# Half of the query projection moved from the last key tile to the second of the query stages

## The chip, the cores and the metric

The kernel runs on one core of one Trainium2 chip. The metric is the device time of one execution in microseconds (us). Before the change it is 979.66 us, the median of three runs (974.97 to 980.01).

## The reference, cut to what matters

One decoder layer, batch B = 2, 1024 tokens, width 256: random-feature attention, then cross attention, then a causal attention with eight chosen experts per head. Each part reads a layer norm of x and adds its result to x. The change lies in the first part:

```python
q = split_heads(x @ Wq.T + bq)
k = split_heads(x @ Wk.T + bk)
v = split_heads(x @ Wv.T + bv)
logits = einsum('bhld,hdf->bhlf', k, W0) - 0.5 * sum(k * k)
alpha = softmax(logits over all L * NF)      # over all tokens and features
N = einsum('bhlf,bhld->bhfd', alpha, v)      # sums of the key features
D = sum(alpha, axis=2)
phi = softmax(einsum('bhld,hdf->bhlf', q, W0))
out = (phi @ N) / (phi @ D + EPS)
```

Sixteen heads of 16 columns, 64 features a head. The query projection `x @ Wq.T + bq` gives a 256 x 1024 matrix for each batch.

## The kernel before, in words

The program has a hand-written order for each engine, and semaphores between them. For each of the two batches (loop over b) the first attention runs so:

- Key projection: `projection` (L1101 to L1107) makes one piece n of four (256 columns of output in two halves, 1024 tokens in two chunks of 512). A piece is two float32 matmuls of 128x512, which the profile shows as four instructions.
- Key tiles, t = 0 to 7 (from L1147): the features of 128 keys (L1153), their values (L1161), some of the squares of the keys (L1167, one semaphore `kk_ps` at the end of tile 7), and, by the table `QUERIES_AT` (L243), pieces of the query projection (L1171 to L1175): piece 0 with tile 3, piece 1 with tile 4, pieces 2 and 3 with tile 7. All four use bank 7 of PSUM, so a piece waits until ScalarE has moved the one before out of it (`until(pe, "q_sb", b, n)`).
- VectorE takes maxima and subtracts them (L834, L842). After tile 7's maxima it makes the weights of the keys (L824, L825), GpSimd takes a maximum across the partitions (L498), VectorE subtracts it (L849), ScalarE takes exp (L616), and VectorE multiplies the values by the weights in two parts (L880; the first part covers ten heads).
- ScalarE moves the projections into `kqT` and adds the bias in `biased` (L568 to L573; the activation is L572). Inside the key loop (L610 to L620) it moves the first piece of a tile ahead of the exp L616, the second behind the exp L618 of the same tile. `kqT` lies in the tile that the profile calls region.
- Query stages, s = 0 to 25 (L1193). In stage s TensorE makes the features f of query tile s (L1207), turns the exp of the tile before (L1222), multiplies the tile two back by the sums (L1255), and so on down a chain of lags. Stages 0 and 1 also hold the sums of the key features, N and D, in two halves of 64 matmul instructions each (L1239). L1239 waits for the exp of all key tiles and for its part of the weighted values.
- In stage 2 the sums are put in place. ScalarE copies them (L649), TensorE turns them (L1214), then turns the exp of query tile 1 (L1222), VectorE copies the turned sums into windows (L889, L891, six copies, semaphore `n_blk`), TensorE multiplies them by a small block (L1228, `za_ps`), VectorE adds that (L922, `n_ready`), and TensorE may begin L1255 for query tile 0. VectorE has the subtraction L914 of query tile 2 between the last copy and L922.
- Query tiles 0 to 3 need pieces 0 and 1; query tiles 4 to 7, from stage 4 on, need all four (L1197).
- ScalarE in a stage: the copy of the turned exp (L656, by the helper L548), then the exp of this stage's query tile (L640, `features_exp`). In the first batch it also rounds two expert pieces in stages 2 and 3 (L548, `expert_hi`).

Of the kernel before, what the change touches and what calls it, by code (L numbers as in the profile page):

```python
# [5 lines left out]
def decoder_layer(nc: bass.Bass, d, out: bass.AP):  # L6
# [54 lines left out]
    SUMMED = [(0, 0), (0, 1), (0, 2), (1, 0), (1, 1), (0, 3), (1, 2), (1, 3)]  # L61
    SUMMED += [(e, p) for e in range(2, E3) for p in range(PAIRS3)]
    LAST_OF = {e: max(n for n, (x, _) in enumerate(SUMMED) if x == e) for e in range(E3)}
    GW = G + H3

    ctx = ExitStack()
    with ctx:
        def sb(name, shape, dt=fp32):
            return ctx.enter_context(nc.sbuf_tensor(name, shape, dt))
# [3 lines left out]
        WkT, WqT, WvT, WoT = (sb(n, [P, DA, D]) for n in ("WkT", "WqT", "WvT", "WoT"))  # L73
# [37 lines left out]
        def view(words):  # L111
            v = region[:, at[0]:at[0] + words]
            at[0] += words
            assert at[0] <= REGION, at
            return v
# [12 lines left out]
        kqT = view(DA * S).rearrange("p (a s) -> p a s", a=DA)  # L128
# [85 lines left out]
        def until(eng, name, b, k):  # L214

            if b * PER[name] + k > 0:
                eng.wait_ge(sem[name], b * PER[name] + k)
# [22 lines left out]
        TURN_AT = {3 * t + 9: t for t in range(TT)}  # L240

        SQUARES_AT = {1: range(0, 2), 2: range(2, 6), 5: range(6, 10), 6: range(10, 14), 7: range(14, 16)}
        QUERIES_AT = {3: (0,), 4: (1,), 7: (2, 3)}  # L243
        OFFSET = (0, 10)
        VALUES_AT = OFFSET[1] + TT + 1
        LAST = VALUES_AT + TT
# [20 lines left out]
        def due(s, lag):  # L267

            return [(a, s - OFFSET[a] - lag) for a in range(2) if 0 <= s - OFFSET[a] - lag < TT]
# [276 lines left out]
        def _(act):  # L546
            def copy(dst, src, name):
                act.activation(dst, src, ACT.Copy).then_inc(sem[name], 1)  # L548

            def norm_apply(b, a, t):  # L550

                i, idx = t % 4, a * TT + t
                until(act, "shift_ready", b, idx + 1)
                if idx >= 2:
                    until(act, "xnT_ps", b, idx - 1)
                act.activation(xn[:, t % 2, :], X[:, b, t, :], ACT.Identity, bias=shift[:, i, 0:1],
                               scale=rstd[:, i, 0:1]).then_inc(sem["xn_ready"], 1)

            def norm_evac(b, a, t):

                until(act, "xnT_ps", b, a * TT + t + 1)
                if a == 2:
                    act.activation(wide_hi[:, :, t * P:(t + 1) * P],
                                   ps[:, 7, 0:D].rearrange("p (a s) -> p a s", a=DA), ACT.Copy)
                copy(xT[:, :, t * P:(t + 1) * P],
                     ps[:, row_bank(b, a, t), 0:D].rearrange("p (a s) -> p a s", a=DA), "xT_ready")

            def biased(dst, n, bank, col, ready, name, b):  # L568

                c, half = n // 2, n % 2  # L570
                until(act, ready, b, n + 1)
                act.activation(dst[:, half, c * CH:(c + 1) * CH], ps[:, bank + n % 2, :], ACT.Identity,  # L572
                               bias=cols[:, col + half:col + half + 1]).then_inc(sem[name], 1)  # L573

            def piece_high(b, q):

                g = b * PIECES + q
                act.wait_ge(expert_in, 16 * (g + 1))
                if SLOTS <= q < E3 + SLOTS:
                    piece_used(act, b, q - SLOTS)  # L580
                if q >= SLOTS:
                    act.wait_ge(piece_kept[q % SLOTS], 32 * (q // SLOTS))
                copy(expert_hi[:, g % SLOTS, :], expert[:, :], "piece_hi")
# [21 lines left out]
            for b in range(B):  # L605
# [4 lines left out]
                for t in range(TT):  # L610
                    queries = QUERIES_AT.get(t, ())
                    for n in queries[:1]:
# [23 lines left out]
                def features_exp(a, t):  # L636

                    wide, scale = (H1 * NF, 1.0) if a == 0 else (K2, SCALE2)
                    until(act, "f_sub", b, a * TT + t + 1)
                    act.activation(phi[:, t % 2, 0:wide], phi[:, t % 2, 0:wide], ACT.Exp,  # L640
                                   scale=scale).then_inc(sem["f_exp"], 1)

                for s in range(LAST):
                    if b == 0 and s in (2, 3):
                        piece_high(b, s - 2)
                    if s == 1:
                        features_exp(0, 1)
                        until(act, "n_ps", b, 2)
                        copy(N1T, ps[:, 4, :], "n_sb")  # L649
                    for a, t in due(s, 1):  # L650
                        until(act, "fT_ps", b, a * TT + t + 1)
                        if t >= 2:
                            until(act, "num_ps", b, a * TT + t - 1)
                        i = t % 2
                        if a == 0:
                            copy(phT[:, i, :], ps[:, 0:2, :].rearrange("p a s -> p (a s)"), "fT_sb")  # L656
                        else:
                            act.activation(phT[:, i, 0:CH], ps[:, 0, :], ACT.Copy)
                            copy(phT[0:K2L, i, CH:CH + P], ps[0:K2L, 1, 0:P], "fT_sb")
                    for a, t in due(s, 0):  # L660
                        if s != 1:
                            features_exp(a, t)
                    for a, t in due(s, 3):
                        until(act, "cxT_ps", b, a * TT + t + 1)
                        if t >= 2:
                            until(act, "y_ps", b, a * TT + t - 1)
                        copy(cxT[:, t % 2, :, :], ps[:, 4, 0:D].rearrange("p (a s) -> p a s", a=DA), "cxT_sb")
                    for a, t in due(s, 5):
                        norm_apply(b, a + 1, t)
                    for a, t in due(s, 6):  # L670
                        norm_evac(b, a + 1, t)
                        if a == 0 and t % TC == TC - 1:
                            for n in range(2 * (t // TC), 2 * (t // TC) + 2):
                                biased(kqT, n, 2, 4, "q2_ps", "q2_sb", b)
                    if s in GATES_AT:
                        gates(GATES_AT.index(s))
                    if 0 <= (t := s - VALUES_AT) < TT:

                        until(act, "val_ps", b, t + 1)
                        copy(V3_heads[:, t], ps[:, t % 4, :].rearrange("p (a i k) -> p a i k", i=2, k=HD3), "val_a")  # L680
# [388 lines left out]
        def _(pe):  # L1069
# [31 lines left out]
            def projection(n, bank, w, name):  # L1101

                c, half = n // 2, n % 2
                for i in range(DA):
                    last = mm(ps[:, bank + n % 2, :], w[:, i, half * P:(half + 1) * P],  # L1105
                              xT[:, i, c * CH:(c + 1) * CH], start=(i == 0), stop=(i == DA - 1))
                last.then_inc(sem[name], 1)  # L1107
# [25 lines left out]
            for b in range(B):  # L1133
# [13 lines left out]
                for t in range(TT):  # L1147
# [21 lines left out]
                    if t == max(SQUARES_AT):  # L1169
                        last.then_inc(sem["kk_ps"], 1)  # L1170
                    for n in QUERIES_AT.get(t, ()):  # L1171
                        if b + n == 0:
# [20 lines left out]
                for s in range(LAST):  # L1193
# [22 lines left out]
                    for a, t in due(s, 1):  # L1216
# [6 lines left out]
                                                phi[:, t % 2, k * P:k * P + r], ident)  # L1223
                        last.then_inc(sem["fT_ps"], 1)
                    if s == 2:
                        until(pe, "n_blk", b, 2 * len(N1_RUNS))
                        for k0, k1, w0 in N1_RUNS:
                            last = mm(ps[:, 6, 2 * k0:2 * k1], eps_blk,  # L1228
                                      N1w[:, k0:k1, w0 + HD1:w0 + 2 * V1W:V1W], start=True, stop=True)
                        last.then_inc(sem["za_ps"], 1)  # L1230
                    if s < 2:

                        until(pe, "e_ready", b, TT)
                        until(pe, "wv_ready", b, s + 1)
                        for u in range(s * PAIRS1 // 4, (s + 1) * PAIRS1 // 4):
                            for t in range(TT):
                                for v in range(2):
                                    c0, p = (t * PAIRS1 + 2 * u + v) * 2 * V1W, 2 * u + v
                                    last = mm(ps[v * HALF:(v + 1) * HALF, 4, u * P:(u + 1) * P],  # L1239
                                              V1_all[:, c0:c0 + HALF], E1[:, t, p * P:(p + 1) * P],  # L1240
                                              start=(t == 0), stop=(t == TT - 1))
                        last.then_inc(sem["n_ps"], 1)
# [259 lines left out]
```

## Time and profile before

| | |
|---|---|
| three timed runs | 974.97, 980.01, 979.66 us; median 979.66 |
| the profiled execution | 980.92 us, its span 979.1 us |
| TensorE matmul busy | 938.1 us, 96% of the span |
| VectorE / ScalarE / GpSimd busy | 682.1 / 390.3 / 236.5 us |
| mean granted TensorE clock | 0.994 of full |
| share of TensorE in the chain that ended last | 79% |

The durations of the trace are those of one execution. The span begins with its first instruction; the profiled execution took 1.8 us more than its span. A time such as 57.81 is counted from the span's start. The first batch passes the changed place at 51 to 75 us, the second at 530 to 555 us. A granted clock of 1.00 is 2.4 GHz, 0.50 is 1.2 GHz.

### The profile page before, as it was taken

The page shows a single profiled execution, that of the slowest core. Times are in us where ns is not written, and L with a number is a line of the kernel's source. Part 1 is how long each engine was busy: PE and PEld are TensorE (multiplying, and loading weights), DVE is VectorE, ACT ScalarE, POOL GpSimd, SP SyncE. Part 2 cuts the span into 40 slices and gives each one's busy share as a digit, 9 for nine tenths or more (in the row PEclk, how much of TensorE's full clock was granted, in tenths as well). Part 3 has the DMA queues.
Part 4 walks back from the last instruction along what each step waited for, and adds up shares of the span by engine and source line. Part 5 has one row for each costly group of instructions (what it writes and reads, how often), then busy time and mean ns, then how long its engine had stood idle before and what let it go on. Part 6 is the DMA issues. An engine that isn't in the chain of part 4 may idle for free.

```text
span 979.1 us, 14699 instructions
## 1 busy us (share of the span) xinstructions
PE 938.1 (96%) x5620; PEld 730.3 (75%) x5620; DVE 682.1 (70%) x1054; ACT 390.3 (40%) x680; POOL 236.5 (24%) x253
## 2 busy tenths in 40 slices
PE   6889999999999999999999998999999999999998
PEld 3668778887756655789976785888876656659998
DVE  3767566547557867988868475765574777879887
ACT  3644555130466766401023355630205655761000
POOL 6212412222533312136610032300032101411000
PEclk9999999999999999999999899999999999999999
DMA  8003000433245511255630000023121000022753
GB/s 257 26 25 127 1 1 1 148 117 129 65 150 185 182 63 45 60 172 178 179 123 1 1 1 2 1 60 119 46 88 39 23 22 0 22 76 84 206 178 125
DMA packets 33739, 81.56 MB, mean 83 GB/s; under 512 B 5847, under 2 KB 10551, under 8 KB 33671
## 3 DMA queue, kind: packets, MB, share of 16 engines
q1 hardware_dynamic: 32391, 76.44, 24.8%
q10 hardware_dynamic: 1280, 4.20, 1.6%
q8 instruction: 45, 0.74, 0.3%
q14 instruction: 23, 0.19, 0.1%
HBM read 61.26 MB, written 19.20 MB: 82 GB/s over the span
## 4 chain that ended last, share of the span: by engine, by line
PE 79%; DVE 10%; ACT 4%; DMA 3%; issue 3%; POOL 1%; ACTq 0%; SPq 0%; DVEq 0%; POOLq 0%
PE ps L1097 18%; PE ps L1403 10%; PE ps L1340 8%; PE ps L1255 5%; PE ps L1409 5%; PE ps L1300 5%; PE ps L1105 4%; PE ps L1316 3%; PE ps L1207 3%; PE ps L1269 3%; DVE region L989 3%; PE ps L1222 2%; PE ps L1376 2%; PE ps L1377 2%; PE ps L1239 1%
## 5 line engine op out<-in xcount | busy, mean ns | idle before, releaser
L1340 PE MATMUL ps<-region 128*128 128x512 f32 (+3 forms) x384 | 161.4, 503 | 0.0
L968 DVE TENSOR_REDUCE region<-ps 128x1 f32<-128x512 f32 (+1 forms) x192 | 98.2, 551 | 64.1 <-PE ps L1319 64.1
L749 ACT ACTIVATE region<-ps 128x512 f32<-128x512 f32 x192 | 92.2, 486 | 122.7 <-PE ps L1379 110.7
L1013 DVE COPY_PREDICATED region<-region,ps 128x512 f32<-128x512 uint32 x112 | 82.0, 736 | 72.0 <-PE ps L1097 71.4
L1403 PE MATMUL ps<-expert_hi,kst 128*128 128x256 f32 x512 | 125.1, 282 | 4.1 <-DVE kst L1043 2.2
L1403 PE MATMUL ps<-expert_lo,kst 128*128 128x256 f32 x512 | 123.3, 279 | 0.0
L1097 PE MATMUL ps<-expert_hi,wide_hi 128*128 128x512 f32 x256 | 102.7, 401 | 0.0
L548 ACT ACTIVATE region<-ps 64x512 f32<-64x512 f32 (+4 forms) x146 | 80.8, 556 | 50.2 <-PE ps L1222 23.1
L1097 PE MATMUL ps<-expert_hi,wide_lo 128*128 128x512 f32 x256 | 100.2, 391 | 0.0
L1403 PEld LDWEIGHTS ps<-expert_hi,kst 128*128 128x128 f32 x512 | 96.0, 187 | 5.3 <-DVE kst L1043 2.6
L1097 PE MATMUL ps<-expert_lo,wide_hi 128*128 128x512 f32 x256 | 99.8, 390 | 0.0
L1403 PEld LDWEIGHTS ps<-expert_lo,kst 128*128 128x128 f32 x512 | 96.5, 189 | 0.0
L1043 DVE TENSOR_TENSOR kst<-region 128x1024 fp32r<-128x1024 f32 x64 | 78.5, 1227 | 19.7 <-PE ps L1409 19.6
L1376 PE MATMUL ps<-qq,kst 128*128 128x512 f32 x192 | 86.6, 451 | 2.3 <-ACT region L749 2.0
L420 POOL TENSOR_TENSOR qx<-region,qq 64x1024 fp32r<-64x1024 f32 x16 | 41.4, 2585 | 195.9 <-ACT qq L548 195.7
L1316 PE MATMUL ps<-kst,qq 128*128 128x512 f32 (+1 forms) x192 | 79.7, 467 | 4.4 <-DVE region L968 4.4
L1409 PE MATMUL ps<-expert_hi,qq 128*128 128x256 f32 x512 | 72.5, 279 | 0.0
L1340 PEld LDWEIGHTS ps<-region 128*128 128x128 f32 x384 | 64.4, 193 | 6.1
L1377 PE MATMUL ps<-qx,kx 128*128 128x512 f32 x192 | 66.4, 346 | 0.0
L1409 PEld LDWEIGHTS ps<-expert_hi,qq 128*128 128x128 f32 x512 | 65.3, 188 | 0.0
L409 POOL TENSOR_TENSOR expert_lo<-expert,expert_hi 128x1024 fp32r<-128x1024 f32 x16 | 39.0, 2437 | 101.2 <-ACT expert_hi L548 101.2
L907 DVE TENSOR_REDUCE top<-ps 128x8 f32<-128x512 f32 (+1 forms) x64 | 34.2, 577 | 36.5 <-PE ps L1207 36.5
(148 smaller groups left out, 1782.7 us busy)
## 6 DMA issues: line engine op xcount, KB each, us to landing
region<-hot_rows SPq DMA_DIRECT2D x128, 128.0 KB, 3.4
expert_hi<-halves_kept SPq DMA_DIRECT2D x24, 512.0 KB, 3.7
expert_lo<-halves_kept SPq DMA_DIRECT2D x24, 512.0 KB, 5.0
halves_kept<-expert_hi SPq DMA_DIRECT2D x16, 512.0 KB, 5.2
halves_kept<-expert_lo SPq DMA_DIRECT2D x16, 512.0 KB, 5.9
expert<-in_value_experts SPq DMA_DIRECT2D x8, 512.0 KB, 4.2
expert<-in_output_experts SPq DMA_DIRECT2D x8, 512.0 KB, 4.3
gb<-gate_rows ACTq DMA_DIRECT2D x16, 256.0 KB, 3.9
```

The costliest lines, as they stand in the source:

```text
L548: act.activation(dst, src, ACT.Copy).then_inc(sem[name], 1)
L749: act.activation(PT[:, g % RING, lo:CH], ps[:, 4 + g % 2, 0:CH - lo], ACT.Exp).then_inc(sem["pt_ready"], 1)
L968: dve.tensor_reduce(mx[:, i, at_mx:at_mx + 1], ps[:, max_bank(h, m), 0:w], AX.X, ALU.max).then_inc(sem["s_max"], 1)
L1013: dve.copy_predicated(V3_heads[:, t], chosen.unsqueeze(3).broadcast_to([P, PAIRS3, 2, HD3]), ps[:, n % 4, :].rearrange("p (a i k) -> p a i ...
L1043: dve.tensor_tensor(kst[i][:, :], oT[:, p, :], masks[:, n % MASKS, :], ALU.mult).then_inc(sem["mo_hi_ready"], 1)
L1097: last = mm(ps[:, n % 4, :], x[:, i, rows_of], columns(w, i), start=(k == 0), stop=(k == len(parts) - 1))
L1316: last = mm(ps[:, max_bank(h, m), 0:w], qq[i][:, t * P:(t + 1) * P], kst[i][:, c * CH:c * CH + w], start=True, stop=not diagonal)
L1340: mm(ps[:, SUM_BANK[c], lo:CH], V3[:, j, h // 2, h % 2 * HD3:(h % 2 + 2) * HD3], PT[:, g % RING, lo:CH], start=(j == 0), stop=(j == TC * ( ...
L1376: mm(ps[:, bank, 0:w], kst[i][:, key], qq[i][:, query], start=True, stop=False)
L1377: last = mm(ps[:, bank, 0:w], kx[i][:, key], qx[i][:, query], start=False, stop=j < TC * c)
L1403: mm(ps[:, 4 + t // 2, t % 2 * D:(t % 2 + 1) * D], kst[n % 2][:, t * P:(t + 1) * P], w[:, slot, columns], start=(n == 0 and t % 2 == 0 and ...
L1409: return mm(ps[:, 4 + t // 2, t % 2 * D:(t % 2 + 1) * D], qq[n % 2][:, t * P:(t + 1) * P], expert_hi[:, slot, columns], start=False, stop= ...
```

## The change

Pieces 2 and 3 of the query projection, and the two ScalarE activations that move them out, leave key tile 7. On TensorE piece 2 now stands in stage 2 between the turning of query tile 1's exp (L1222) and L1228, piece 3 between L1228 and L1255. On ScalarE the two activations stand in stage 2 before and behind `features_exp` of query tile 2. Bank 7 is used as before, sizes and counts are the same, in both batches.

```diff
-        QUERIES_AT = {3: (0,), 4: (1,), 7: (2, 3)}
+        QUERIES_AT = {3: (0,), 4: (1,)}
...
+                    if s == 2:
+                        biased(kqT, 2, 7, 0, "q_ps", "q_sb", b)
                     for a, t in due(s, 0):
                         if s != 1:
                             features_exp(a, t)
+                    if s == 2:
+                        biased(kqT, 3, 6, 0, "q_ps", "q_sb", b)
...
                         last.then_inc(sem["fT_ps"], 1)
                     if s == 2:
+                        until(pe, "q_sb", b, 2)
+                        projection(2, 7, WqT, "q_ps")
                         until(pe, "n_blk", b, 2 * len(N1_RUNS))
                         for k0, k1, w0 in N1_RUNS:
                             last = mm(ps[:, 6, 2 * k0:2 * k1], eps_blk,
                                       N1w[:, k0:k1, w0 + HD1:w0 + 2 * V1W:V1W], start=True, stop=True)
                         last.then_inc(sem["za_ps"], 1)
+                        until(pe, "q_sb", b, 3)
+                        projection(3, 6, WqT, "q_ps")
```

## Rows read from the trace of the kernel before

**Rows 1.** The page, part 1: busy time, share of span, instructions of each engine.

```profile
PE 938.1 (96%) x5620; PEld 730.3 (75%) x5620; DVE 682.1 (70%) x1054; ACT 390.3 (40%) x680; POOL 236.5 (24%) x253
```

**Rows 2.** Chain of waits, first batch, key tile 7 to sums: start us, us, what.

```profile
51.23 0.43 PE ps L1167 x4
...
52.51 2.40 issue
54.90 0.40 POOL region L498
...
56.09 1.59 DVE region L880
...
57.81 3.71 PE ps L1239 x64
```

**Rows 3.** Timeline of PE, first batch: start us, us, instruction, count, [idle before <-releaser].

```profile
51.48 1.91 PE L1105 MATMUL ps<-xT,WqT 128*128 128x512 f32 x4
54.17 1.99 PE L1105 MATMUL ps<-xT,WqT 128*128 128x512 f32 x4 [0.78 <-ACT region L572]
...
68.96 1.06 PE L1222 MATMUL ps<-const,region 128*128 128x128 f32 x8
71.00 0.83 PE L1228 MATMUL ps<-region,const 128*128 128x2 f32 x6 [0.97 <-DVE region L891]
72.62 3.08 PE L1255 MATMUL ps<-region 128*128 128x102 f32 x16 [0.79 <-DVE region L922]
```

**Rows 4.** Chain of waits, second batch.

```profile
531.02 1.76 PE ps L1105 x4
...
533.54 1.99 PE ps L1105 x4
...
536.59 3.64 PE ps L1239 x64
...
551.33 3.71 PE ps L1255 x16
```

**Rows 5.** Timeline of DVE, second batch.

```profile
532.93 0.28 DVE L849 TENSOR_TENSOR region<-region 128x128 f32<-128x128 f32 x1
533.13 0.42 DVE L852 TENSOR_TENSOR region<-ps,rows 128x256 f32<-128x256 f32 x1
533.82 2.50 DVE L880 TENSOR_TENSOR region<-region 128x1360 f32<-128x1360 f32 x2 [0.27 <-ACT region L616]
```

**Rows 6.** Timeline of ACT, second batch.

```profile
532.80 0.69 ACT L572 ACTIVATE region<-ps,cols 128x512 f32<-128x512 f32 x1 [2.63 <-PE ps L1105]
533.39 0.30 ACT L616 ACTIVATE region<-region 128x128 f32<-128x128 f32 x1
```

**Rows 7.** Timeline of ACT, first batch, stage 2.

```profile
70.06 1.02 ACT L548 ACTIVATE region<-ps 128x1024 f32<-128x1024 f32 x1 [0.30 <-PE ps L1222]
72.30 1.06 ACT L640 ACTIVATE region<-region 128x1024 f32<-128x1024 f32 x1 [1.21 <-DVE region L914]
```

**Rows 8.** Stretches: length, busy PE, PEld, DVE, ACT, POOL; granted clock, DMA share, GB/s.

```profile
34.00:37.30 3.30, 1.16 (x6) 0.68 (x5) 3.30 (x7) 3.16 (x10) 2.16 (x1) 1.00 0.07 10
69.90:72.62 2.72, 0.96 (x9) 0.78 (x7) 2.42 (x10) 1.35 (x2) 2.30 (x1) 1.00 0.00 0
72.62:77.29 4.67, 4.67 (x25) 3.98 (x26) 0.68 (x2) 1.56 (x2) 0.00 (x0) 0.63 0.81 261
548.70:551.33 2.63, 0.87 (x8) 0.78 (x7) 2.35 (x9) 1.35 (x2) 0.00 (x0) 0.97 0.00 0
551.33:558.55 7.22, 7.22 (x34) 6.21 (x35) 2.14 (x5) 0.73 (x1) 0.00 (x0) 0.54 0.01 2
```

**Rows 9.** Chain of waits, first batch, stages 3 and 4.

```profile
78.31 1.76 PE ps L1255 x16
...
80.29 1.06 PE ps L1207 x8
81.36 1.02 PE ps L1222 x8
```

## The prediction

> **What bounds the kernel now.** I read the page first. Matmuls are busy for 96% of the span [rows 1], so the end is set by TensorE, and a microsecond counts where TensorE waits or where its matmuls run long. The chain of waits says where that is around the change. In the first batch the chain leaves TensorE at the last square of key tile 7 (51.23 + 0.43 = 51.66) and comes back only at 57.81 with the sums L1239; 2.40 us of it is GpSimd not yet starting, then come L498, the subtraction, an exp, and 1.59 us of L880 [rows 2]. The two query pieces that are to move lie beside that chain, not in it [rows 3]. In the second batch the chain runs through both pieces and the features of query tile 0, up to 536.59 [rows 4]: there TensorE itself is late. Next I read the timeline at stage 2. TensorE ends L1222 at 70.02, idles 0.97 us, runs six tiny matmuls (0.83 us), idles 0.79 us and begins L1255 at 72.62 [rows 3]: 2.60 us with almost no work. The second batch has the same stretch before 551.33, the numbers within 0.03 us. Last I read the granted clock. At both places, and nowhere else before the end of the span, it falls to 0.50, which is 1.2 GHz: the mean is 0.63 over 72.62 to 77.29 and 0.54 over 551.33 to 558.55 [rows 8]. Behind each near-empty stretch the work is slow.
>
> **The price of the low clock.** L1255, L1207 and L1222 take 1.76 + 1.06 + 1.02 = 3.84 us at full clock [rows 9]. After 551.33 the same 32 instructions take 7.22 us [rows 8], 3.38 more. After 72.62 they take until 78.31 [rows 9], 5.69 us or 1.85 more. Both falls together cost 5.2 us. The fastest timed run is 5.95 us under the profiled execution, which is what a run without them would show; but no trace of that run exists.
>
> **What the change removes from key tile 7.** Eight matmul instructions (1.91 and 1.99 us busy) and two activations per batch.
> First batch: the sums wait for the chain over GpSimd, which holds neither a piece nor an activation, so they begin at 57.81 as before: gain 0. The pieces were hidden there. If they go, TensorE makes the features of query tile 0 at once (51.66 to 52.72, with 1.06 from [rows 9]) and then has nothing for 57.81 - 52.72 = 5.09 us.
> Second batch: the exp L616 now waits behind the activation of piece 2, which began at 532.80 and ran 0.69 [rows 6], while its input was there at 532.93 + 0.28 = 533.21 [rows 5]. Without it L616 ends near 533.55, which is also when VectorE is done with L852 (533.13 + 0.42). L880 then starts at 533.57 instead of 533.82. From the start of L880 to the sums is 57.81 - 56.09 = 1.72 us in the first batch [rows 2], so the sums begin at 535.29, not 536.59: gain 1.30. The gap before them: features done at 531.02 + 1.06 = 532.08, so 3.21 us idle. L618, the last exp that the sums need, stands right behind L616; in the first batch the chain names L880 and not it as the last before the sums [rows 2], and I take the same here.
>
> **What it adds to stage 2.** First batch, by its clock: piece 2 takes 1.76 us [rows 4], 70.02 to 71.78. The turned sums are in place at 71.00 [rows 3], so their wait is covered. L1228 runs to about 72.6. ScalarE is free from 71.08 [rows 7]; it moves piece 2 at 71.80 to 72.49, so piece 3 finds its bank free when L1228 ends, and runs to 74.4. VectorE's L922 (0.3 us) comes at about 72.7, beside piece 3. L1255 begins at 70.02 + 1.76 + 0.83 + 1.76 = 74.37, against 72.62: loss 1.75. Bounds: 1.4, if the weight loads of L1228 hide behind piece 2; 2.0, if piece 3 takes the 1.99 that it takes when begun from idle [rows 4]. I take 1.75, since piece 2 runs without a pause before it. The second batch has the same stretch: 1.75 again.
> The new wait on ScalarE stands ahead of the exp of query tile 2, which would start at 72.5 instead of 72.30 [rows 7]. TensorE wants that exp after L1255 and L1207, at 74.37 + 2.8 = 77.2; it ends at 73.6. Cost 0, cover 3.6 us. The activation of piece 3 (74.4 to 75.1) is wanted in stage 4. No DMA is issued by the moved step, and nothing is moved past a queue of SyncE or GpSimd.
>
> **What it does to the clock.** With 3.5 us of wide matmuls in stage 2, both near-empty stretches vanish, and with them the falls: gain 1.85 + 3.38 = 5.23. But two gaps open ahead of the sums. Both are emptier and longer (5.09 and 3.21 us) than the stretches of 2.6 us that preceded the falls. The other side is the stretch from 34.00 to 37.30: 2.14 us of it empty, and the clock stayed at 1.00 [rows 8]. I take it that both gaps bring a fall. Its price is 0 at best (all the low time falls into the gap) and 3.38 at worst by the rows; I take 1.85, the lower of the two measured, for each, since part of the low time passes while TensorE has nothing to run. Everything behind a gap (12.2 us of matmuls in the first batch up to 70.02) is TensorE's own work, so a slow stretch there is lost in full.
> The Trainium skill ("TensorE: Matmul & The Clock Gate", Part 1 and the section on oscillation) says that the reduced clock is the default which activity lifts, and that a kernel should leave TensorE no long idle gaps. That rule speaks against this change: by it the two new gaps both cost, which is the sum as I make it (+0.7), and without it the sum would be -3.0. The rows go further than the rule, since the stretches before the two falls were not idle but held small matmuls. The page also says that the moment of a fall is not tied to the kernel; no single trace can show that.
>
> **The sum**, against the profiled execution (980.92 us): -1.30 + 1.75 + 1.75 - 5.23 + 1.85 + 1.85 = +0.67 us. The profiled execution lies 1.26 us above the median of the runs; I carry the difference over: 979.66 + 0.7 = 980.4 us. Without anything of the clock the change would be +2.2.
>
> **The rivals.**
> 1. *Fewer falls.* The second gap (3.21 us), or both, leave the clock at 1.00, as the 2.14 us before 37.30 did. Then -1.2 or -3.0: 978.5 or 976.7. For it: stretches of 2 to 3 us went both ways in the trace, and one timed run looks free of falls. Against: the new gaps are longer and quite empty.
> 2. *The low clock outlasts the gap* (the slower side). Place: L1239 in stages 0 and 1. Its weights are only 64 wide, and after 551.33 the clock stayed low through the 3.71 us of L1255 [rows 4] and beyond. If the sums don't either, 12.2 us of work from 57.81 to 70.02 runs at half speed: +12.2 in one batch, in place of 1.85, gives +11.0, 990.7. It decides once the two gaps cost over 7.9 us together. Against: neither fall of the trace lasted longer than 7 us.
> 3. *The start of the sums does not move* in the second batch, since another wait stands in (L618 or L852 late). Then +2.0: 981.6.
> 4. *More than I see.* GpSimd starts L498 2.40 us late in the first batch [rows 2]; in the second VectorE has no wait ahead of L849 [rows 5]. Should the 2.40 us go with the pieces, and no gap bring a fall, -5.4: 974.3. Nothing in the rows ties it to TensorE.
>
> **How the numbers follow.** Forecast, both gaps bring a short fall: 0.45, own range 979.0 to 982.5. Rival 1: 0.33. Rival 2: 0.09. Rival 3: 0.08. Rival 4: 0.05. About 0.5% or 4.9 us is what a measurement can tell from no change, and only rival 2 in full and rival 4 pass it, with a little for falls at other moments than in the profiled run. Faster 0.06, same 0.83, slower 0.11. The range goes from rival 1 with no fall (976.7, less the lower end 1.4 of each stage 2, hence 976.0) to two falls at 3.38 each and 2.0 in each stage 2 (+4.2, hence 984.0).
>
> **What would show it.** Right: sums at 57.8 in the first batch and 1.3 us earlier in the second; a gap of about 5 and 3 us with clock 0.50 behind it; 4.4 us from L1222 to L1255 in stage 2 with clock 1.00 behind it. Wrong: a clock of 1.00 through both gaps, a clock still at 0.50 when stage 2 begins, or a wait of TensorE ahead of piece 3.

## The result, and the profile after

The changed kernel takes 982.36 us (median of 19 runs, 979.15 to 984.02), the kernel before 978.65 us (19 runs, 974.97 to 980.77). The ratio is 1.0033, 95% interval 1.0023 to 1.0043: slower by 3.2 us, between 2.3 and 4.2. That is under the 0.5% taken as no change, but it is not zero. The profiled execution took 982.52 us, its span 980.7 us, its mean granted clock 0.995. Medians and ratios here and below leave out five executions, taken with the experiments, that ran 1161 to 2537 us. (Lines of kernel.py have moved: projection L1105 is L1109, sums L1239 are L1247, L1255 is L1263, L1222 is L1226, L1228 is L1234, L880 is L884.)

The chain of waits of the changed kernel, first batch (start us, us, what), answers to [rows 2]:

```profile
53.47 0.43 PE ps L1171 x4
...
54.75 2.56 issue
57.32 0.40 POOL region L498
...
58.51 1.59 DVE region L884
...
60.23 5.13 PE ps L1247 x64
...
73.87 1.73 PE ps L1109 x4
75.60 0.02 issue
75.62 0.70 ACT region L572
76.32 0.04 issue
76.36 1.99 PE ps L1109 x4
78.35 1.76 PE ps L1263 x16
```

From the last square (53.90) to the sums it is 6.33 us, 6.15 before: nothing is gained, as forecast. (All of it comes 2.2 us later than in [rows 2] for reasons ahead of the change: the start was 0.65 us later, and after the wait at 38 us the clock fell in this execution, which cost 1.6 us.) The first half of the sums takes 5.13 us in place of the 3.64 to 3.71 it takes at full clock. In stage 2 it is 4.48 us from the end of L1226 to L1263, against 2.60, and the move of piece 2 by ScalarE stands in the chain.

The same view in the second batch, for [rows 4]:

```profile
533.33 0.43 PE ps L1171 x4
...
536.42 1.59 DVE region L884
538.00 0.14 issue
538.14 5.11 PE ps L1247 x64
...
551.75 1.73 PE ps L1109 x4
...
553.51 0.70 ACT region L572
554.20 0.04 issue
554.25 1.99 PE ps L1109 x4
556.23 1.76 PE ps L1263 x16
```

The sums start 4.38 us behind the last square, against 536.59 - 531.02 = 5.57 before: 1.19 gained, 1.30 forecast.

The stretches, for [rows 8]: length, then busy time of PE, PEld, DVE, ACT, POOL, then the granted clock. Gap ahead of the sums, first half of the sums, and the work behind stage 2, in each batch:

```profile
53.90:60.23 6.33, 1.06 (x8) 0.64 (x9) 4.21 (x8) 1.26 (x2) 0.39 (x1) 0.96 0.00 0
60.23:65.36 5.13, 5.13 (x66) 4.96 (x66) 3.17 (x5) 1.06 (x1) 0.00 (x0) 0.71 0.01 3
78.35:82.19 3.84, 3.84 (x34) 3.36 (x34) 1.65 (x4) 1.75 (x2) 0.39 (x1) 1.00 0.93 367
533.76:538.14 4.38, 1.05 (x9) 0.63 (x9) 4.12 (x8) 1.25 (x2) 0.39 (x1) 0.94 0.00 0
538.14:543.25 5.11, 5.11 (x66) 4.94 (x66) 3.17 (x5) 1.06 (x1) 0.00 (x0) 0.72 0.01 3
556.23:560.08 3.85, 3.85 (x35) 3.38 (x34) 1.66 (x4) 0.69 (x1) 0.00 (x0) 1.00 0.02 4
```

The low clock has changed its place: 0.71 and 0.72 at the sums, 1.00 behind stage 2. Each fall comes inside the new gap, shortly before its end (0.96 and 0.94 there), and lasts into the sums.

### The profile page after: what moved, and what is told of

Same layout as the page of the kernel before. It is cut to its first block, busy times and chain, and to the rows that moved or that the text cites. A ratio compares the mean times of both kernels' runs of the same rounds, so it can differ in the third digit from the quotient of the medians.

```text
span 980.7 us, 14699 instructions
## 1 busy us (share of the span) xinstructions
PE 936.8 (96%) x5620; PEld 730.8 (75%) x5620; DVE 683.4 (70%) x1054; ACT 390.4 (40%) x680; POOL 236.1 (24%) x253
## 4 chain that ended last, share of the span: by engine, by line
PE 80%; DVE 10%; ACT 4%; issue 3%; DMA 2%; POOL 0%; ACTq 0%; SPq 0%; DVEq 0%; POOLq 0%
PE ps L1101 18%; PE ps L1411 9%; PE ps L1348 8%; PE ps L1417 5%; PE ps L1308 5%; PE ps L1109 4%; PE ps L1263 4%; PE ps L1324 3%; PE ps L1211 3%; PE ps L1277 3%; DVE region L993 3%; PE ps L1226 3%; PE ps L1384 3%; PE ps L1385 2%; PE ps L1247 2%
```

## The experiments

Two theories. Mine: the price is 1.7 us in each stage 2 and a fall of the clock at each new gap, against 1.2 us gained in the second batch and the falls behind stage 2 that no longer happen. The rival: the clock is a side show, and one half of the change alone makes the loss.

**Each half alone.** `r1_removed_alone` leaves pieces 2 and 3 out: they are not computed, and query tiles 4 to 7 use what is in their place (the semaphore counts follow).

```diff
-        QUERIES_AT = {3: (0,), 4: (1,), 7: (2, 3)}
+        QUERIES_AT = {3: (0,), 4: (1,)}
```

> Only the removal: pieces 2 and 3 of the query projection are not computed at all (query tiles 4 to 7 then use what the keys left there), stage 2 is as before. My theory (sums of the second batch 1.2 us earlier; each new gap costs about 1.4 us by the low clock; the near-empty stretch of stage 2 stays and still costs by the clock in some runs): +0.5 to +2.5 us against before, sums start at 4.4 us behind the last square in the second batch, clock 0.50 right behind the gap. Rival (the gap is harmless, the loss is all in stage 2): -1.2 us, clock 1.00 at the sums.

`r2_added_alone` keeps them in tile 7 and computes them a second time in stage 2, by the added lines of the change.

> Only the addition: pieces 2 and 3 stay in key tile 7 and are computed a second time in stage 2. My theory: 1.9 us more per batch from L1222 to L1255 in stage 2, less the falls of the clock there: +3.8 us less 0 to 5.2, by the spread of the runs before about +1 to +3 us; no low clock behind stage 2, and none at the sums. Rival (stage 2 hides the pieces, the loss comes from the gaps): -3 to -5 us.

Measured: removal 1.0015 (1.0003 to 1.0026), or +1.5 us; addition 1.0026 (1.0010 to 1.0043), or +2.6 us. Both halves lose. In the trace of the removal the sums start 1.1 us earlier in the second batch and take 6.59 and 5.38 us for their first half. Its first batch (timeline of PE, what it idled for in brackets):

```profile
59.37 6.59 PE L1239 MATMUL ps<-region 128*64 128x128 f32 x64 [5.12 <-DVE region L880]
...
75.43 0.83 PE L1228 MATMUL ps<-region,const 128*128 128x2 f32 x6 [0.97 <-DVE region L891]
77.06 2.00 PE L1255 MATMUL ps<-region 128*128 128x102 f32 x16 [0.80 <-DVE region L922]
```

6.59 us is 2.9 more than at full clock: the longest price seen at a gap. The near-empty stretch of stage 2 brought no fall in this batch; in the second it did (L1255 took 2.94 us there). In the trace of the addition the clock is 1.00 throughout the kernel, so in that trace nothing is lost by the clock: its cost is stage 2 itself and something at the end (below).

**The clock held up by matmuls that nobody reads.** `r3_before_warm` puts them into the idle spots of stage 2 of the kernel before, `r4_after_warm` into the gaps of the changed kernel. I call them fillers. (Excerpts of both edits; the comments are added here to say where a line stands.)

```diff
+            def filler(n, wide=CH):
+
+                for _ in range(n):
+                    mm(ps[:, 7, 0:wide], WqT[:, 0, 0:P], xT[:, 0, 0:wide], start=True, stop=True)
...
+                        filler(1)                      # r3, ahead of the wait for n_blk
...
+                        filler(1, CH // 2)             # r3, behind L1228
...
+                        filler(3 if b else 5)          # r4, ahead of the sums
```

> The kernel before with idle time of stage 2 filled by matmuls whose results nobody reads: one of 128x512 ahead of the wait for the turned sums, one of 128x256 behind L1228. Nothing waits for them. My theory: L1255 begins as before (2.6 us behind L1222), the clock never falls behind stage 2: 1 to 3 us faster than before, and the spread of the runs is smaller. Rival (the low clock of the traced run is rare or costs nothing on average): 0.

> The changed kernel with the gap ahead of the sums filled by matmuls whose results nobody reads (five of 128x512 in the first batch, three in the second). My theory: no fall of the clock at the sums, L1247 takes 3.7 us in place of 5.1: 2.9 us faster than the changed kernel, so about +0.8 us against before. Rival (the gaps cost nothing by the clock): as the changed kernel, +3.7 us.

The local part came out as the theory has it. In `r4_after_warm` both gaps carry matmuls, and the first half of the sums takes 3.71 us again, at clock 1.00 in both batches:

```profile
53.56 4.56 PE L1116 MATMUL ps<-xT,WqT 128*128 128x512 f32 x10
59.10 3.71 PE L1255 MATMUL ps<-region 128*64 128x128 f32 x64 [0.98 <-DVE region L884]
```

```profile
59.10:62.80 3.70, 3.70 (x66) 3.53 (x66) 3.17 (x5) 0.49 (x1) 0.00 (x0) 1.00 0.02 4
535.28:539.00 3.72, 3.72 (x66) 3.55 (x66) 3.17 (x5) 0.52 (x1) 0.00 (x0) 1.00 0.02 4
```

The time is 1.0001 of the kernel before (0.9988 to 1.0014): 3.1 us better than the change itself (1.0033), and 2.5 us better than its second measurement (1.0027, below). This shows that the low clock at the gaps is a real part of the loss. `r3_before_warm` has no fall behind stage 2 either, but gave only 0.9993 (0.9977 to 1.0009), where 1 to 3 us were expected: not told apart from zero; part of the reason is a later wait (below). These two kernels also give the price of the moved pieces free of the clock: from the first sums matmul to the first projection of the cross attention it is 50.20 us in `r4_after_warm` (59.10 to 109.30) and 48.54 in `r3_before_warm` (58.92 to 107.46), so 1.66, and the second batch has 50.19 against 48.55. First `r4_after_warm`, then `r3_before_warm`:

```profile
109.30 3.70 PE L1109 MATMUL ps<-xT,W2q 128*128 128x512 f32 x8 [0.47 <-ACT xT L548]
```

```profile
58.92 3.71 PE L1247 MATMUL ps<-region 128*64 128x128 f32 x64 [1.01 <-DVE region L880]
...
107.46 3.70 PE L1105 MATMUL ps<-xT,W2q 128*128 128x512 f32 x8 [0.47 <-ACT xT L548]
```

**The wait ahead of piece 3.** `r5_piece3_other_bank` writes it to bank 4, with a wait for its move ahead of the first use of that bank in stage 3.

```diff
-                        biased(kqT, 3, 6, 0, "q_ps", "q_sb", b)
+                        biased(kqT, 3, 3, 0, "q_ps", "q_sb", b)
...
-                        until(pe, "q_sb", b, 3)
-                        projection(3, 6, WqT, "q_ps")
+                        projection(3, 3, WqT, "q_ps")
...
+                        if a + t == 0:
+                            until(pe, "q_sb", b, 2 * NC)
```

> The changed kernel with piece 3 written to bank 4 of PSUM, which is free in stage 2, so that it need not wait until ScalarE has moved piece 2 out of bank 7. My theory (the 0.2 us that TensorE idles ahead of piece 3, and its start from idle, are the wait for that move): L1222 to L1255 takes 4.3 us in place of 4.48, in both batches. Rival (L1228 or something else holds piece 3): 4.48 as before. The time of one run can't show 0.4 us.

The chain of waits of that run, stage 2 of the first batch:

```profile
72.20 1.72 PE ps L1109 x4
73.92 0.56 PE ps L1234 x6
74.48 1.82 PE ps L1109 x4
76.30 1.76 PE ps L1262 x16
```

4.10 us (4.11 in the second batch) in place of 4.48; ScalarE has gone from the chain. The wait was the shared bank. It was an error of the prediction, which had piece 3 find its bank free.

**The kernel before, traced again.**

> The kernel before, unchanged, traced a second time. My theory: the falls of the clock behind stage 2 are not in every execution, since the medians put their mean cost at 1 to 2 us and not at the 5.2 us of the first trace; of the four near-empty stretches of stage 2 traced so far three had a fall. Expected: one or both batches without a fall or with a shorter one, so a cost under 5.2 us. Rival (they come every time, 1.9 and 3.4 us): 0.5 in the same stretches, 5.2 us.

This execution took 983.31 us, alone and so without an interval. Both stretches of stage 2 had a fall again, shorter in the second batch than in the first trace (stretches from L1255 to the next L1255):

```profile
73.80:79.60 5.80, 5.80 (x35) 4.91 (x36) 1.75 (x4) 1.85 (x3) 0.74 (x1) 0.71 0.84 271
555.18:560.90 5.72, 5.72 (x34) 4.93 (x35) 1.67 (x4) 0.74 (x1) 0.00 (x0) 0.70 0.01 3
```

From L1255 to the cross projection it took 35.35 us in both batches, against 33.73 where the clock stays up, so 1.6 and 1.6 us lost: under 5.2, as expected, though the falls themselves were not rarer than in the first trace. The clock also fell at two places where it stayed up in the first trace: behind the wait at 36 us, and at 433 us, behind a wait of 2.22 us for an expert piece.

**Half of the change, placed in the idle spots.** `r7_half_moved` leaves piece 2 in tile 7 and puts the two matmuls of piece 3 one into each idle spot of stage 2. Everything is computed.

```diff
-        QUERIES_AT = {3: (0,), 4: (1,), 7: (2, 3)}
+        QUERIES_AT = {3: (0,), 4: (1,), 7: (2,)}
...
+                    if s == 2:
+                        biased(kqT, 3, 6, 0, "q_ps", "q_sb", b)
...
+                        until(pe, "q_sb", b, 3)
+                        projection(3, 6, WqT, "q_ps", (0,))
                         until(pe, "n_blk", b, 2 * len(N1_RUNS))
...
                         last.then_inc(sem["za_ps"], 1)
+                        projection(3, 6, WqT, "q_ps", (1,))
```

> Only piece 3 leaves key tile 7, piece 2 stays. In stage 2 the two matmuls of piece 3 stand one ahead of the wait for the turned sums and one behind L1228, each 0.88 us, where TensorE idled 0.97 and 0.79 us. My theory: sums of the second batch 1.1 us earlier as with both pieces gone; stage 2 at most 0.2 us longer per batch and never a low clock behind it; the gap of the first batch shrinks to 3.3 us, of the second to 1.4 us, so a fall at the sums in the first batch at most (1.4 us). Against before: -0.8 plus 1.4 less about 1.3 for the falls of stage 2, -2 to 0 us. Rival (any query work in stage 2 costs its full length): +1 to +2 us.

976.41 us, 0.9971 of the kernel before (0.9959 to 0.9983): 2.8 us faster where 0 to 2 were expected, and faster than both kernels of this study. The timeline of PE, first batch:

```profile
72.76 1.06 PE L1225 MATMUL ps<-const,region 128*128 128x128 f32 x8
73.66 1.02 PE L1107 MATMUL ps<-xT,WqT 128*128 128x512 f32 x2
74.79 0.83 PE L1233 MATMUL ps<-region,const 128*128 128x2 f32 x6
75.48 1.10 PE L1107 MATMUL ps<-xT,WqT 128*128 128x512 f32 x2
76.42 1.99 PE L1261 MATMUL ps<-region 128*128 128x102 f32 x16
```

L1261 begins 2.60 us behind L1225 (73.82), as L1255 did before: 1.8 us of matmuls cost nothing there. The clock behind it is 1.00 in both batches. The stretches around the sums, with the first half of the sums in line 1 and the gap of the second batch in line 2:

```profile
60.40:65.50 5.10, 5.10 (x66) 4.93 (x68) 3.09 (x5) 1.06 (x1) 0.00 (x0) 0.75 0.01 3
...
531.90:537.10 5.20, 3.49 (x20) 1.81 (x19) 4.64 (x9) 1.83 (x3) 0.39 (x1) 1.00 0.00 0
```

The first batch still pays for a fall (1.3 us); the second, with 1.7 us idle, does not, and its sums start 1.0 us earlier than before.

`r8_mixed` keeps the first batch as before with fillers in stage 2, and has piece 3 moved in the second only. `r9_half_warm` is `r7_half_moved` with three fillers in the gap of the first batch.

> First batch as before, with matmuls nobody reads in the two idle spots of stage 2; second batch as in the run with half moved. My theory: no gap over 1.5 us ahead of the sums, no low clock at the sums or behind stage 2 in either batch, second sums 1.1 us earlier: -1.0 us less about 1.3 for the falls, -1 to -3.5 us against before. Rival (keeping the clock up is worth nothing on average): -1.0 us.

> The kernel with half moved, and three matmuls of 128x512 that nobody reads in its gap of 3.3 us ahead of the sums of the first batch. My theory: no low clock at the sums of either batch, the first sums half takes 3.7 us in place of 5.0: 1.3 us faster than with half moved alone, -3.5 to -4.5 us against before. Rival (the fall in that gap is rare over many executions): as with half moved, -2.9 us.

> The kernel with half moved once more, on the same chip as its neighbours. Theory: -2.9 us against before again, its interval clear of zero, and some 6 us under the changed kernel of this call. Rival (the first -2.9 was a lucky chip or placement): -1 to 0 us.

> The changed kernel once more. Theory: +3.3 us against before; in the trace low clock behind both gaps (5.1 us for the first sums half), none behind stage 2, 4.48 us from L1226 to L1263. Rival (falls in the gaps depend on the execution): one of the two gaps at 1.00.

`r8_mixed`: 0.9985 (0.9975 to 0.9995), or -1.5 us, too near to both theory (-1 to -3.5) and rival (-1.0) to decide. `r9_half_warm`: 0.9999 (0.9989 to 1.0009); its sums had clock 1.00 in both batches, and yet the 1.3 us did not come: neither theory gave this number. `r10_half_again`: 0.9981 (0.9967 to 0.9994), median 976.99 us, so the half move is faster a second time, by 1.9 us and not the 2.9 expected; it is 4.4 us under the changed kernel taken beside it, where some 6 were expected. `r11_after_again`: 1.0027 (1.0013 to 1.0041), 981.34 us. In the trace of `r11_after_again` both gaps bring a fall again, and the sums pay more for it than in the first trace:

```profile
59.46 6.08 PE L1247 MATMUL ps<-region 128*64 128x128 f32 x64 [5.41 <-DVE region L884]
...
537.74 5.38 PE L1247 MATMUL ps<-region 128*64 128x128 f32 x64 [3.33 <-DVE region L884]
```

**Why fillers give less than they should.** From the first output-expert matmul of the second batch to the last, the five kernels with more matmul instructions than before (r2, r3, r4, r8, r9) took 94.1 to 96.0 us, the eight traces without 91.4 to 92.7. In the chain this is one fetch. First `r3_before_warm`, then the kernel before (chain of waits):

```profile
897.88 8.11 DMA expert_lo<-halves_kept
```

```profile
901.92 6.10 DMA expert_lo<-halves_kept
```

TensorE waited 2.9 us for it, against 0.9 before (2.0 to 2.2 in r2, r4, r8 and r9), and in r3, r4, r8 and r9 the clock fell 0.6 to 1.5 us behind the end of that wait, in none of the other traces there. So these four kernels keep the clock up early and lose it once late. `r13_added_elsewhere` adds a single matmul at a spot far from the change:

```diff
                     until(pe, "out_ready", b - 1, TC)
+                    filler(1, CH // 2)
```

> The kernel before with one matmul of 128x256 (two instructions) that nobody reads, in the second batch between the key projection and the key tiles, where TensorE idles 0.8 us and the clock stays at 1.00. In all five traces with added matmul instructions the last output stretch of the second batch took 94.1 to 96.0 us, in all eight without them 91.4 to 92.7, since one fetch of an expert piece landed late there. If added instructions as such bring that (theory): 94 us or more in that stretch and a median at or above before. Rival (it has to do with the clock or the time at which the stretch is reached): 92.4 us, and the median of before.

It took 1.0016 (1.0000 to 1.0032) of the kernel before, 0.6 us of which is the matmul itself: TensorE idles 0.78 us ahead of it as before, so it stands behind the gap and not in it. The fetch took 6.73 us and the stretch 93.1: between the two groups, so neither theory. That added instructions bring the late fetch is not shown; what does is open.

## Why the prediction was right, and where it was off

The range (976.0 to 984.0) and the likeliest class (within 0.5%) held; the sum was low: +0.7 us forecast, +3.2 measured. The band of the likeliest class is 9.8 us wide and the range 8.0, against a miss of 2.5 in the sum, so that they held says little for the sum. By its steps:

- *First batch, start of the sums: 0.* Held (6.33 against 6.15 us, the difference being GpSimd's 2.56 in place of 2.40). Rival 4 fell: that delay did not go away with the pieces (6.0 to 6.6 us in all fourteen traces, with them or without).
- *Second batch: -1.30.* Measured -1.19 by the chain, -1.1 by the starts of the matmuls. Held. Rival 3 fell.
- *Stage 2: +1.75 each.* 1.66 each by `r4_after_warm` against `r3_before_warm`. The size held, by two errors that cancel: piece 3 does wait for its bank and begins from idle (4.48 us, not 4.35), but L1263 then follows without a pause and is through sooner than when it begins from idle.
- *New gaps: +1.85 each.* Of the eight gaps with both pieces gone (two each in the profile after, r1, r5, r11) all eight brought a fall, 3.3 us idle or more each. By the first half of the sums they cost 1.4, 2.9, 1.4 and 2.4 us in the first batch, and 1.4, 1.7, 1.4 and 1.7 in the second: 3.5 us together in the mean, 3.7 forecast. Rival 1 (no fall) did not occur in the changed kernel. Rival 2 (the low clock outlasts the sums) did not occur either: 2.9 us was the longest price.
- *Falls behind stage 2: -5.23.* This is the term that failed: the falls did go, but they were worth less. It was read from one execution, and the sum was then carried to the median as if that execution were typical. From L1255 to the cross projection takes 33.7 us with no fall; in three traces of this stage 2 (before, r6, r13) the two batches lost 4.8, 3.2 and 4.8 us together, 4.3 in the mean (this measure leaves out the 0.2 us that L1255 takes longer for being begun from idle). `r1_removed_alone` has this stage 2 too and lost 1.6; with it the mean is 3.6. And the timed executions have more clock than the traced ones: mean granted clock 0.9956 over the runs of the kernel before taken with the experiments, against 0.994, 0.993 and 0.995 in these three traces. 0.0016 of 977 us is 1.6 us, so I put the falls of a timed run at about 2.7 us. That part is worked out, not shown: the mean clock does not tell where a fall was, and in these 100 runs 0.001 of clock goes with 0.7 us, not with 1.0. The size is not known better than to about 1 us.

With the measured sizes: 2 x 1.66 - 1.1 + 3.5 - 2.7 = +3.0 us, against +3.2 (2.3 to 4.2). Without the clock the change costs 2.2 us by the traces, as the prediction said; the timed runs of r4 and r3 lie only 0.8 us apart, with intervals of 1.3 and 1.6 either way, and so neither confirm nor refute it. The half move fits too: -1.0 for the sums, about 2.0 for a fall in the one gap left (1.3 and 2.8 us in its two traces), -2.7 for stage 2, -1.7 us against -2.8 and -1.9 measured. So does the removal: -1.1 + 3.5 = +2.4, against +1.5 (0.3 to 2.5). The kernels with added matmuls fit only roughly, even with what their last stretch took beyond the 92.4 us before: r2 +2.3 against +2.6 measured, r8 -0.8 against -1.5, r9 -0.3 against -0.1, but r3 +0.9 against -0.7 and r4 +2.3 against +0.1.

The rule of the Trainium skill ("TensorE: Matmul & The Clock Gate", Part 1) that activity keeps the full clock up and a gap costs it: the traces agree, 8 falls in 8 gaps, and none where matmuls filled them. The measurement goes further than the page where it speaks of idle gaps: seven of eight stretches of 2.6 us that held six small matmuls brought a fall too. Of the shorter idle gaps, 2.1 us before the first query piece brought one in 6 of 14 traces, and the 1.7 us that the half move leaves in the second batch in none of four.

## What to carry to other kernels

Work moved into a wait is free only as far as it fits: split it by the waits (0.97 and 0.79 us here, one matmul each) rather than by its own units; two whole pieces cost 1.66 us a batch, the one split piece nothing. (A single piece left whole in one spot was not run, so how much of this is the split and how much the smaller load is open.) Ask what the moved work covered where it stood: hidden matmuls were what kept TensorE's clock up through a wait for another engine. And read a term that hangs on the clock from several executions, since it comes and goes by microseconds between runs of the same program.

## What was not expected of the hardware

The stretch at 35 to 38 us of the first batch, 2.14 us idle ahead of the first query piece, had the clock at 1.00 behind it in the first trace of the kernel before, but fell in 6 of the 14 traces, for 1.6 us each time (13.77 us from that piece to the last square without it, 15.4 with it). No edit touched it. At the same place of the same instructions the clock falls in one execution and not in the next. And the fetch of one expert piece took 5.5 to 6.2 us in the seven chains that hold it of kernels without added matmuls and 6.7 to 8.1 in the six with them, a difference as large as the change under study, with its cause open.
